# Second attention of a four-layer kernel: the steps of its order cut in two, one piece of the other products in each

## What is computed

```python
x = x + _L0_attn_ref(_layernorm(x), wq, wk, wv, wo)            # linear attention
x = x + _L0_ffn_ref(_layernorm(x), gate_w, wg, wu, wd, ...)    # 8 experts, two a token, and a shared one
x = x + _L1_attn_ref(_layernorm(x), Wq, bq, Wk, bk, Wv, bv, Wp, bp)
x = x + _L1_ffn_ref(_layernorm(x), W1, W2, Wg, bg)             # 8 experts, one a token

# _L1_attn_ref
energy = jnp.einsum('bhqd,bhkd->bhqk', q, k)
energy = jnp.where(jnp.abs(idx[:, None] - idx[None, :]) > 128, fmin, energy)
att = jax.nn.softmax(energy / jnp.sqrt(256.0), axis=-1)
out = jnp.einsum('bhqk,bhkd->bhqd', att, v)
return jnp.einsum('bne,fe->bnf', out.transpose(0, 2, 1, 3).reshape(B, N, E), Wp) + bp
```

## Time and profile before

| what | value |
|---|---|
| three runs | 1651.01, 1659.97, 1661.58 us, median 1659.97 |
| the profiled execution | 1662.55 us |
| its span, first to last instruction | 1660.8 us |
| outside the span | 1.75 us |
| mean granted TensorE clock | 0.934 |
| busy share of the span | PE 90%, weight loads 60%, DVE 44%, ACT 27%, POOL 27% |

### The profile page before, as it was taken

One profiled execution on the slowest core, in us unless ns is written; L12 is line 12 of the kernel. 1 busy time (PEld: TensorE's weight loads), 2 busy tenths in 40 slices (PEclk: granted clock), 3 DMA queues, 4 the chain that ended last, 5 costly groups with the idle time before them and its releaser, 6 DMA issues.

```text
span 1660.8 us, 22693 instructions
## 1 busy us (share of the span) xinstructions
PE 1493.7 (90%) x7115; PEld 997.7 (60%) x7115; DVE 734.8 (44%) x2378; ACT 446.4 (27%) x763; POOL 450.0 (27%) x533
## 2 busy tenths in 40 slices
PE   5999999999999999828899999999997279999998
PEld 3666655565777777515556666666664247667775
DVE  4354323462333333227667867867661422222221
ACT  1111111111111121103455555545543011111111
POOL 1000000003622222142444544444222033333332
PEclk8899999999999999957899999999996589999999
DMA  9200010001112212143444544534423911111110
GB/s 340 60 26 13 26 38 0 1 1 42 61 61 64 63 59 65 46 118 103 130 118 123 160 117 124 160 108 127 141 59 122 335 45 48 46 49 47 49 48 23
DMA packets 87809, 139.73 MB, mean 84 GB/s; under 512 B 10094, under 2 KB 52208, under 8 KB 87697
## 3 DMA queue, kind: packets, MB, share of 16 engines
q1 hardware_dynamic: 73856, 105.60, 20.5%
q0 software_dynamic: 12096, 32.13, 6.7%
q10 hardware_dynamic: 1744, 0.55, 0.1%
HBM read 86.46 MB, written 52.17 MB: 83 GB/s over the span
## 4 chain that ended last, share of the span: by engine, by line
PE 79%; DMA 7%; ACT 5%; DVE 3%; SPq 3%; issue 2%; POOL 1%; ACTq 0%; POOLq 0%; DVEq 0%
PE psum L632 11%; PE psum L514 10%; PE psum L831 8%; PE psum L807 8%; PE psum L611 6%; PE psum L525 5%; PE psum L680 4%; PE psum L703 4%; DMA strips<-hi 4%; PE psum L730 4%; ACT arena L989 3%; PE psum L658 3%; DMA qT<-strips 2%; PE psum L818 2%; PE psum L441 2%
## 5 line engine op out<-in xcount | busy, mean ns | idle before, releaser
L1442 DVE CUSTOM_DVE_ANT_0 work<-psum,mask 128x384 bf16<-128x384 f32 (+1 forms) x512 | 227.7, 487 | 108.7 <-PE psum L658 107.9
L989 ACT ACTIVATE arena<-psum 128x512 f32<-128x512 f32 (+1 forms) x256 | 178.1, 703 | 197.1 <-PE psum L680 196.8
L1539 POOL DMA_INDIRECT work<-normed,token_of x110 | 104.6, 951 | 416.8 <-PE psum L593 207.3
L632 PE MATMUL psum<-arena,work 128*128 x568 | 186.5, 471 | 2.9 <-ACT work L912 2.4
L658 PE MATMUL psum<-kz,qT 96*128 96x384 f32 (+1 forms) x512 | 157.1, 382 | 32.0 <-DMA qT<-strips 23.8
L514 PE MATMUL psum<-arena 128*128 128x512 f32 (+1 forms) x384 | 176.4, 602 | 0.0
L680 PE MATMUL psum<-qT,kz 100*128 100x384 f32 (+1 forms) x512 | 138.8, 347 | 28.2 <-ACT arena L989 28.1
L658 PEld LDWEIGHTS psum<-kz,qT 96*128 96x128 f32 x512 | 88.0, 198 | 94.9 <-issue 38.7
L831 PE MATMUL psum<-arena,work 128*128 x312 | 143.3, 603 | 1.2 <-ACT work L912 1.2
L807 PE MATMUL psum<-arena,work 128*128 x624 | 141.2, 379 | 1.9 <-DVE work L1494 1.9
L632 PEld LDWEIGHTS psum<-arena,work 128*128 128x128 f32 x568 | 102.9, 191 | 54.2 <-issue 5.7
(11 more groups left out here) (170 smaller groups left out, 2093.9 us busy)
## 6 DMA issues: line engine op xcount, KB each, us to landing
strips<-hi SPq DMA_DIRECT2D x64, 256.0 KB
arena<-in_w SPq DMA_DIRECT2D x16, 1024.0 KB, 12.6
kz<-strips SPq DMA_DIRECT2D x64, 192.0 KB, 3.1
qT<-strips SPq DMA_DIRECT2D x32, 384.0 KB, 4.6
results<-work SPq DMA_DIRECT2D x71, 128.0 KB, 1.7
normed<-work SPq DMA_DIRECT2D x16, 512.0 KB, 3.4
strips<-lo SPq DMA_DIRECT2D x32, 256.0 KB
X<-in_x SPq DMA_DIRECT2D x8, 512.0 KB, 9.9
```

The source lines that it names most:

```text
L632: m = e.matmul(psum[:, pair[u], 0:INTER], xsT0[:, b % 2, c * P:(c + 1) * P], wu0[:, bass.ds(x, 1), c, u * INTER:(u + 1) * INTER], start=(c ...
L989: e.activation(pT[:, j, 2 * half:2 * half + 2, 0:w], src, ACT.Exp, scale=1.0 / E ** 0.5).then_inc(p_exped, 1)
L1442: e.tensor_tensor_reduce(masked[:, n % 2, 0:w], psum[:, bank_of["scores", u, i, hd], at:at + w], mask[:, P - off:P - off + w], 1.0, MASKED ...
L1539: e.indirect_dma_start(out=xs[:, b % 3, :], out_offset=None, in_=normed[l], in_offset=bass.IndirectOffsetOnAxis(ap=token_of[:, l, b:b + 1] ...
```

## The change

A unit now has 8 steps and a batch 32 (`UNIT`, `BATCH`). A step holds the scores of two heads of one tile, the transposed scores of two heads of another tile, and then at most what else is due; the second half of a tile has a step of its own. Before, one step held both halves, with all other products between them. Due times are renumbered; most are twice the old ones, give or take a few. The norms go one tile a step. In `act_attention` and `dve_attention` the work on the other products stands behind the work on the heads, `dve_low` stands ahead of `dve_v`, and the fetched outputs are added four new steps earlier. In SP's loop the keys and queries of a unit (`sp_place`) are due at step -8 from its start, where they were at -3 of the old steps; the maxima are due at +8, before at +4.

```diff
 NU = B * NG
-PRE = 4 * NG
-FIRST_STEP, LAST_STEP = -PRE - 6, 4 * NU + 24
+UNIT = 2 * TPB
+BATCH = UNIT * NG
+FIRST_STEP, LAST_STEP = -48, BATCH * (B - 1) + 76
+AGAIN_AT = 14
...
-    u, i = divmod(step - first, 4)
+    u, i = divmod(step - first, UNIT)
     return [(u, i)] if 0 <= u < NU and i < n else []
...
-    b, i = divmod(step - first, PRE)
+    b, i = divmod(step - first, BATCH)
...
-    return spread(step, (-7, -5, 1, 3))
+    return spread(step, (-13, -10, 3, 6))
...
-    return spread(step, (-6, -2, 2, 6))
+    return spread(step, (-12, -4, 4, 12))
...
-    return spread(step, (29, 31))
+    return spread(step, (58, 62))
...
-    return [(u, 0) for u, _ in unit(step, 10, 1)] + [(u, 1) for u, _ in unit(step, 12, 1)]
+    return [(u, 0) for u, _ in unit(step, 21, 1)] + [(u, 1) for u, _ in unit(step, 25, 1)]
...
         def pe_attention(e):
             for s in range(FIRST_STEP, LAST_STEP):
-                for u, i in unit(s, 0, 4):
-                    pe_scores(e, u, i, 0)
-                for u, j in unit(s, 7, 4):
-                    pe_again(e, u, j, 0)
-                for u, _ in unit(s, 14, 1):
+                for u, i in unit(s, 0, UNIT):
+                    pe_scores(e, u, *divmod(i, 2))
+                for u, i in unit(s, AGAIN_AT, UNIT):
+                    pe_again(e, u, *divmod(i, 2))
+                for u, i in values_due(s):
+                    pe_values(e, u, 2 * i)
+                    pe_values(e, u, 2 * i + 1)
+                for u, _ in unit(s, 28, 1):
                     pe_out_rows(e, u)
                 for b, t in qk_due(s):
                     pe_qk(e, b, *divmod(t, 2))
                 for b, t in v_due(s):
                     pe_v(e, b, t)
-                for b, _ in batch(s, -9):
+                for b, _ in batch(s, -17):
                     pe_turn_batch(e, 2, b, M_RING)
-                for b, _ in batch(s, 28):
+                for b, _ in batch(s, 55):
                     pe_project(e, b, 0)
                     pe_project(e, b, 1)
                 for b, half in residual_due(s):
                     pe_residual(e, b, half)
-                for b, _ in batch(s, 36):
+                for b, _ in batch(s, 71):
                     pe_turn_batch(e, 3, b, M_RING)
-                for b, _ in batch(s, 37):
+                for b, _ in batch(s, 74):
                     pe_gate(e, 1, b, xnT[:, NORM[3, b] % 2, :, :], 3, M_RING)
-                for u, i in values_due(s):
-                    pe_values(e, u, 2 * i)
-                    pe_values(e, u, 2 * i + 1)
-                for u, i in unit(s, 0, 4):
-                    pe_scores(e, u, i, 1)
-                for u, j in unit(s, 7, 4):
-                    pe_again(e, u, j, 1)
-                for u, _ in unit(s, 4, 1):
+                for u, _ in unit(s, UNIT, 1):
                     pe_maxima(e, u)
...
         def act_attention(e):
             e.wait_ge(*done["down0", NBLK0 - 1])
             for s in range(FIRST_STEP, LAST_STEP):
-                for u, j in unit(s, 7, 4):
-                    act_exp(e, u, j, 0)
-                for b, t in qk_due(s):
-                    act_high(e, b, *divmod(t, 2))
-                for b, _ in batch(s, -9):
-                    xnT_free(e, 2, b)
-                    act_turned(e, 2, b, xnT[:, NORM[2, b] % 2, 0, :])
-                for b, _ in batch(s, 28):
-                    act_projected(e, b, 0)
-                    act_projected(e, b, 1)
-                for b, _ in batch(s, 36):
-                    xnT_free(e, 3, b)
-                    act_turned(e, 3, b, xnT[:, NORM[3, b] % 2, 0, :])
+                for u, i in unit(s, AGAIN_AT, UNIT):
+                    act_exp(e, u, *divmod(i, 2))
                 for u, i in values_due(s):
                     if i == 1:
                         if u > 0:
                             e.wait_ge(*done["o", u - 1])
                         e.wait_ge(*done["values", u])
                         e.activation(oT, psum[:, O_BANK, :], ACT.Copy).then_inc(oT_made, 1)
...
+                for b, t in qk_due(s):
+                    act_high(e, b, *divmod(t, 2))
...
+                for u, _ in unit(s, UNIT, 1):
                     act_maxima(e, u)
-                for first, norm in ((-11, 2), (33, 3)):
-                    for b, i in batch(s, first, 2):
-                        act_norm(e, norm, b, (2 * i, 2 * i + 1))
-
-        def act_norm(e, norm, b, tiles):
+                for first, norm in ((-25, 2), (65, 3)):
+                    for b, t in batch(s, first, TPB):
+                        act_norm(e, norm, b, t)
...
             for s in range(FIRST_STEP, LAST_STEP):
-                for u, i in unit(s, 4, 1):
+                for u, _ in unit(s, UNIT, 1):
                     dve_maxima(e, u)
-                for u, i in unit(s, 0, 4):
-                    dve_mask(e, u, i, 0)
-                    dve_mask(e, u, i, 1)
-                for u, _ in unit(s, 14, 1):
+                for u, i in unit(s, 0, UNIT):
+                    t, half = divmod(i, 2)
+                    dve_mask(e, u, t, 2 * half)
+                    dve_mask(e, u, t, 2 * half + 1)
+                for u, _ in unit(s, 28, 1):
                     dve_out_rows(e, u)
+                for b, t in qk_due(s):
+                    dve_low(e, b, *divmod(t, 2))
                 for b, t in v_due(s):
                     dve_v(e, b, t)
-                for b, _ in batch(s, -9):
+                for b, _ in batch(s, -17):
                     xnT_free(e, 2, b)
                     dve_turned(e, 2, b, xnT[:, NORM[2, b] % 2, 1, :])
                 for b, half in residual_due(s):
                     dve_residual(e, b, half)
-                for b, _ in batch(s, 36):
+                for b, _ in batch(s, 71):
                     xnT_free(e, 3, b)
                     dve_turned(e, 3, b, xnT[:, NORM[3, b] % 2, 1, :])
-                for b, _ in batch(s, 37):
+                for b, _ in batch(s, 74):
                     dve_gate(e, 1, b)
...
-                for u, i in unit(s, 0, 4):
-                    dve_mask(e, u, i, 2)
-                    dve_mask(e, u, i, 3)
-                for b, t in qk_due(s):
-                    dve_low(e, b, *divmod(t, 2))
-                for b, i in batch(s, -PRE - 3, 2 * TPB):
+                for b, i in spread(s, range(-42, -42 + 4 * TPB, 2)):
                     t, j = b * TPB + i // 2, i % 2
                     dve_add_fetched(e, t, j)
                     if j == 1:
...
                     e.wait_ge(proj_added, 2 * b + i + 1)
                     for t in (2 * i, 2 * i + 1):
                         dve_stats(e, b * TPB + t)
-                for first, norm in ((-12, 2), (32, 3)):
+                for first, norm in ((-27, 2), (63, 3)):
                     for b, _ in batch(s, first):
                         dve_scale(e, norm, b)
...
             for s in range(FIRST_STEP, LAST_STEP):
-                for b, _ in batch(s, -9):
+                for b, _ in batch(s, -20):
...
-                for u, j in unit(s, 7, 4):
+                for u, j in [(u, i // 2) for u, i in unit(s, AGAIN_AT, UNIT) if i % 2 == 1]:
...
-                for b, i in batch(s, -PRE - 6, 2 * TPB):
+                for b, i in spread(s, range(FIRST_STEP, FIRST_STEP + 4 * TPB, 2)):
                     pool_fetch(e, b * TPB + i // 2, i % 2)
-                if s == -11:
+                if s == -22:
                     pool_value_pads(e)
...
             for s in range(FIRST_STEP, LAST_STEP):
-                for u, _ in unit(s, -3, 1):
+                for u, _ in unit(s, -UNIT, 1):
                     sp_place(e, u)
                 for b, t in qk_due(s - 1):
                     sp_keep(e, b, *divmod(t, 2))
-                for u, _ in unit(s, 4, 1):
+                for u, _ in unit(s, UNIT, 1):
                     sp_place_maxima(e, u)
-                for b, _ in batch(s, 31):
+                for b, _ in batch(s, 63):
...
-                for b, _ in batch(s, 34):
+                for b, _ in batch(s, 69):
                     sp_normed(e, 1, b)
...
-                for step, xs in ((7, (0,)), (9, tuple(range(1, NX - 1))), (20, (NX - 1,))):
-                    if s == 4 * NU + step:
+                for step, xs in ((14, (0,)), (18, tuple(range(1, NX - 1))), (40, (NX - 1,))):
+                    if s == UNIT * NU + step:
                         for x in xs:
                             sp_expert(e, x)
```

26 lines of the change are left out of this document (16 added, 10 removed).

## The result

| what | before | after |
|---|---|---|
| median | 1657.09 us (1651.01 to 1661.58) | 1685.86 us (1680.93 to 1692.57) |
| ratio, 95% interval | | 1.0179 (1.0126 to 1.0231) |
| profiled execution, its span | 1662.55, 1660.8 us | 1692.57, 1690.8 us |
| mean granted clock | 0.934 | 0.934 |

Slower by 1.8%; forecast were 1689.0 us and 1.7%.

What follows compares the result with a forecast made beforehand. PE was taken as the bound, busy 58.9 of a batch's 64.0 us. Terms 20.8 - 7.2 + 0 + 15.4 = +29.0 on the profiled 1662.55 gave 1691.5; the median, 2.6 lower, was forecast at 1689.0 us, range 1645 to 1713.

Steps and rivals of the forecast that it cites:

- The maxima behind the second residual: At a unit's start, PE waits 2.4 us once a batch for DVE's maxima, with `dve_scale` put in front.
- R + 3.9: Maxima ready 3.9 us after R, the end of the second residual's matmuls on PE.
- The bank behind the query and key product: Router bank held until `dve_low` ends: PE waits 0.65 us twice and 0.55 us twice a batch.
- The norm and the exponentials: The 1.2 us norm wait before a transpose goes; shorter exponential waits gain 1 to 2 us a batch.
- The mask of step 28: Second head's scores wait for a DVE mask made behind the residual, until 2.7 us after it.
- The first stretch: New steps 0 to 6 of a batch: +2.6 us, to 14.2; +20.8 over eight batches.
- The rival of the clock: Granted clock falls to 0.50 for one more stretch a batch, 25 us in all: 1714 us; chance 0.1.
- The second stretch: New steps 6 to 16 of a batch: -0.9 us, -7.2 over eight batches, slow clock left as it is.
- The third: Stretch of new steps 16 to 22: bank and maxima waits against less for exponentials, 0 in sum.
- The fourth stretch and `max_T`: New steps 22 to 32: maxima land behind SP's load, PE stands 2.3 us; +2.2, seven times +15.4.
- Q: Start of a batch's second query and key product; strips expected at Q + 12.3, PE at step 30 at Q + 15.9.
- the prediction's own rule: On SP's queue, maxima can't be seen before `qT`, issued ahead; the term is +15 with it, +4 without.

Runs made afterwards that it cites:

- before_scale_ahead: The kernel before with the last norm's scale due one old step earlier, ahead of the maxima on DVE: 1654.03 us, ratio 1.0005.
- maxima_one_step_later: The changed kernel with PE's transpose of the maxima and ACT's copy of them one step later, DVE unchanged: 1679.57 us, ratio 1.017.
- low_behind_masks: The changed kernel with `pe_v`, projection and third transpose one step later, and `lo` made behind the next step's masks: 1706.56 us, ratio 1.0313.
- before_low_ahead: The kernel before with DVE making `lo` ahead of the second half's masks instead of behind them: 1656.38 us, ratio 1.0008.

## Why the prediction came out right

- **The maxima behind the second residual** (2.4 us once a batch, 0.6 at two other units). Measured 1.88, and 0.95, 0.64 and 0.69 at the others. The row of L694 was to have 15 to 20 us in 8; in the whole stage it has 32.7 in 29: it waits at all four units of a batch, where the prediction named three and put only one in the row. Two of the smaller waits stand behind DVE's copy of transposes, 0.69 us, as predicted. The one it didn't name, 0.95, stands behind `lo` (0.75) and a fetched output (0.77). That both the DVE order and the missing work on PE are needed was the prediction's reason, and before_scale_ahead bears it out. R + 3.9 was half a microsecond too much: 1081.25 to 1084.69 is 3.4. What the sum had wrong is to count the wait at nearly its full length: with it taken out in maxima_one_step_later, 22.4 us of waits go in 380 and 15.6 come back at the exponentials.
- **The bank behind the query and key product** (0.55 for `pe_v`, 0.65 for the transposes). Measured 0.59, and 0.70 to 0.71. 14.3 us in 22 times.
- **The norm and the exponentials.** The first is gone; the second fell by more than half, 16.9 to 7.4, where the sum had a fifth to a third. The reason is not that pieces hide it better: while PE stands for the maxima or the bank, ACT goes on. maxima_one_step_later shows it the other way round.
- **The mask of step 28** (its scores 2.7 us after the residual). Measured 2.7 (1072.23 to 1074.95), of which 1.49 are the wait.
- **The first stretch** was to be 14.2 us and is 17.0. The missing 2.8 us are the clock: 6.9 us at the lower level, now behind the maxima's wait, cost 3.4, and the maxima's wait is 0.5 shorter. In three batches of five the fall there is only half as long. The rival of the clock had a chance of one in ten and asked for 3.2 us of cost a batch, 25 in the stage. The falls behind waits cost about that, 18.7 us in 380; what it left out is that the falls behind the gate would nearly go (34.0 us of half-clock time before, 6.8 after), so that on balance the clock cost 3.4 us in 380. Nothing in the rows of before showed a fall behind a wait, and that was a poor reason to keep the clock out of the sum.
- **The second stretch** was to lose 0.9 and lost 1.7: here the fall behind the gate is 3.4 us, where it was 6.4. **The third** is 0.5 longer, not 0.
- **The fourth stretch and `max_T`** (+2.2 a batch, +15.4) is the term that failed. The stretch is 20.2, so +1.3, about 9 us, and not from the transfer: PE waited for `max_T` twice in the whole stage, 4.7 us in the first batch and 1.5 later, where seven waits of 2.3 were predicted. It stood for masks, banks and one of the maxima instead. Two steps were off by a microsecond each, and both shortened the wait. The strips, issued at 1066.61, had landed when SP loaded them at 1072.96, Q + 11.0 for Q = 1062.00; the prediction had Q + 12.3. And PE came to step 30 at 1079.01, Q + 17.0 and not Q + 15.9. Together they are the 2.3 us.

PE's second query and key product in the chain of waits:

```profile
1062.00 1.73 PE psum L733 x4
```

SP's timeline behind it:

```profile
1066.61 0.65 SPq L1663 DMA_DIRECT2D strips<-hi  x1
1072.96 0.79 SPq L1676 DMA_DIRECT2D kz<-strips  x2
1074.10 0.30 SPq L1678 DMA_DIRECT2D qT<-strips  x1
1074.46 1.34 SPq L1685 DMA_DIRECT2D qT<-max_T  x2
```

By the prediction's own rule the maxima land with `qT`, at 1074.10 + 4.9 = 1079.0, just when they are wanted. The mechanism was right: low_behind_masks, with the strips later, pays 17.7 us for it in 400.
- **Start and tail** were put at 0. The start is 0, the tail gained 5 us.

The profiled executions differ by 30.0 us (1692.57 less 1662.55) where +29.0 was the sum, but errors cancel in it. By the batch shown, which is 5.5 us longer while the 35 us of the stage make 4.4 on average, the first stretch was 22 us too small in the sum and the third 4, the second was 6 too large, the fourth 6 and the tail 5. The direction and the main row were understood; how near the total came is partly luck. The prediction's count of today's waits, 26 of 380 us, also left out the fourth row, 3.7 us for the strips.

Two things stay open. Why the strips of a batch's last set land in 6.1 to 6.5 us, from the last issue to the load, in most batches of after and in 7.7 to 8.0 before isn't settled. It goes with the place of `dve_low` (6.0 to 6.6 in before_low_ahead, 7.2 to 7.8 in low_behind_masks), and not with the maxima written meanwhile, since in before_low_ahead they are written 3.2 us into the same transfer. And what sends the clock down behind one wait of 1.49 us and not behind the next in the same kernel, and behind the gate in one kernel and seldom in another, wasn't tried by itself.

## What to carry to other kernels

Interleaving more finely on the engine that bounds the kernel helps only if the helper engine has its distance too: count, in order, what it does between the product and the one that is waited for, and put at least as much of the bound engine's own work in between. An even pattern with short steps shortened that distance in front of the maxima, the banks and the masks at once; the old order, with three pairs of each kind and the values in front of the maxima, gave it where it was needed. Move one wait and look at all rows of waits and at the granted clock, not at the row that was to go, since here three mended waits came back under another name (maxima as exponentials, banks as masks, masks as a transfer).

## What the runs showed of the hardware

- The granted clock fell to 0.50 at the end of a 1.88 us stand of PE (1084 to 1091) as well as behind the gate. The same wait of 1.49 us was followed by a fall in four of five batches of one kernel, and the time at that level ranges from 17 to 72 us of 380 between kernels that do the same work in all, one execution of each.
- Executions of one kernel differ by their clock: 0.936 at 1663.29 us and 0.952 at 1640.19.
- The maxima, a small transfer behind a large load on the same queue, landed 3.76 us after their own issue (chain of low_behind_masks).
- From the last issue of a batch's second set of strips to their load 6.0 to 8.0 us go by, by the order of the kernel around it.
